# Cross-attention and FFN: scores and maxima as pairs of 64-row matmuls, operands in projection layout, softmax sums inverted by way of DMA

## The reference

```python
q, k, v = layer_norm(x, g_norm) @ Wq, context @ Wk, context @ Wv      # 16 heads of 64
k, v = [null_k, k], [null_v, v]                                       # 1602 keys
attn = softmax(q @ k.T / 8)                                           # per head, 2048 x 1602
out = layer_norm((attn @ v) @ Wout, g_out)
x = x + out
h = relu(s0 * [y, -y] @ W0) * 2; h = relu(s1 * h @ W1) * 2; h = s2 * h @ W2     # y = layernorm(x)
x = x + h
```

## Time and profile before

| | us |
|---|---|
| runs | 1573.2, 1545.63, 1547.75 (median 1547.75) |
| profiled execution | 1543.19, of it span 1541.2 |
| head, up to the first scores | 128.5 |
| pair 0 / pairs 1 to 6 / pair 7 | 150.1 / 883.1 (147.2 each) / 133.5 |
| tail | 246.0 |
| busy: PE, DVE, POOL, ACT | 1478.7, 1030.3, 779.2, 707.2 |

### The profile page before, as it was taken

The page is one execution under the profiler, slowest core; times in us unless marked ns, Lnnn a source line. Parts: engine busy times, 40 slices in busy tenths (PEclk is TensorE's granted clock), DMA queues, the critical chain, the costliest instruction groups (busy, mean ns, idle before and its releaser), DMA issues.

```text
span 1541.2 us, 20363 instructions
## 1 busy us (share of the span) xinstructions
PE 1478.7 (96%) x6068; PEld 735.0 (48%) x6068; DVE 1030.3 (67%) x1288; ACT 707.2 (46%) x1169; POOL 779.2 (51%) x657
## 2 busy tenths in 40 slices
PE   5888999999999999999999999999999998999998
PEld 3334444444444434444444444444443443878777
DVE  7785677577757866776687578757876838544542
ACT  3324544644464446445544554465445535232242
POOL 3004667566757655666567566656675645101100
PEclk9998999999999999999999999999999999999999
DMA  5222200120020002000200120012002302101000
GB/s 162 76 76 78 57 8 8 34 59 8 11 59 31 8 16 79 8 8 21 72 8 14 25 64 7 15 34 58 8 8 87 123 0 69 55 14 54 14 14 14
DMA packets 46947, 60.23 MB, mean 39 GB/s; under 512 B 4721, under 2 KB 32308, under 8 KB 46836
## 3 DMA queue, kind: packets, MB, share of 16 engines
q1 hardware_dynamic: 46836, 58.92, 12.9%
HBM read 26.27 MB, written 17.30 MB: 28 GB/s over the span
## 4 chain that ended last, share of the span: by engine, by line
PE 89%; DVE 5%; issue 2%; ACT 2%; POOL 1%; DMA 0%; DVEq 0%; SPq 0%; ACTq 0%; POOLq 0%
PE ps_o L1247 26%; PE ps_s L1269 17%; PE ps_s L1270 12%; PE ps_side L1331 10%; PE ps_side L1184 9%; PE ps_side L1172 3%; PE ps_s L1292 3%; PE ps_side L1206 2%; PE ps_side L1162 1%; PE ps_side L1163 1%; DVE mxh L926 1%; PE ps_o L1146 1%; PE ps_side L1193 1%; PE ps_o L1148 1%; DVE khl L915 1%
## 5 line engine op out<-in xcount | busy, mean ns | idle before, releaser
L423 POOL TENSOR_TENSOR acc<-acc,prob 128x512 f32<-128x512 f32 x522 | 670.4, 1302 | 307.5 <-ACT prob L778 300.5
L778 ACT ACTIVATE prob<-ps_s,keybias 128x512 f32<-128x512 f32 x832 | 526.4, 683 | 526.0 <-PE ps_s L1270 482.2
L926 DVE TENSOR_REDUCE mxh<-ps_side 128x2 f32<-128x804 f32 x512 | 485.6, 991 | 122.0 <-PE ps_side L1184 119.2
L1247 PE MATMUL ps_o<-prob,vp 128*64 128x512 f32 x1664 | 448.3, 616 | 0.0
L1269 PE MATMUL ps_s<-qdup,khl 128*128 128x512 f32 x832 | 373.4, 449 | 7.5 <-issue 5.4
L1269 PEld LDWEIGHTS ps_s<-qdup,khl 128*128 128x128 f32 x832 | 156.0, 188 | 364.4 <-issue 261.5
L1270 PE MATMUL ps_s<-qrest,krest 128*128 128x512 f32 x832 | 329.3, 396 | 0.0
L423 DVE TENSOR_TENSOR acc<-acc,prob 128x512 f32<-128x512 f32 x182 | 166.9, 919 | 58.5 <-ACT prob L778 48.5
L1184 PE MATMUL ps_side<-khl,qdup 64*128 64x402 f32 x1024 | 170.5, 401 | 11.5 <-DVE mxh L926 4.3
L1270 PEld LDWEIGHTS ps_s<-qrest,krest 128*128 128x128 f32 x832 | 157.2, 189 | 18.8
L1247 PEld LDWEIGHTS ps_o<-prob,vp 128*64 128x64 f32 x1664 | 84.9, 135 | 140.8 <-issue 81.1
(11 more groups left out here) (130 smaller groups left out, 1041.7 us busy)
## 6 DMA issues: line engine op xcount, KB each, us to landing
qdup<-qdup SPq DMA_DIRECT2D x64, 128.0 KB, 2.3
o_scratch<-onorm SPq DMA_DIRECT2D x32, 256.0 KB, 2.1
otb<-o_scratch SPq DMA_DIRECT2D x4, 2048.0 KB, 7.8
v_scratch<-vsb SPq DMA_DIRECT2D x13, 512.0 KB, 3.2
krest<-khl SPq DMA_DIRECT2D x16, 416.0 KB, 5.1
vp<-v_scratch SPq DMA_DIRECT2D x8, 832.0 KB, 7.4
xs<-in_x SPq DMA_DIRECT2D x4, 512.0 KB, 6.6
xres<-in_x SPq DMA_DIRECT2D x1, 2048.0 KB, 11.1
```

Of the source, the lines that this page charges most:

```text
L423: eng.tensor_tensor(a, so_far, prob[g][s % RING][:, :], ALU.add).then_inc(sum_done[g], 1)
L778: act.activation(prob[g][s % RING][:, :], ps_s[g][:, :], ACT.Exp, bias=keybias[:, kt:kt + 1], scale=SCALE).then_inc(p_made[g], 1)
L926: dve.reduce_max(mxh[:, qt % QH, :, quarter], ps_side[slot][:, :, 0:MXW], AX.X).then_inc(side_free[slot], 1)
L1247: last = pe.matmul(ps_o[qb % 2][hi_rows(g), :], vp[u][:, kt, hi_rows(g)], prob[g][s % RING][:, :], start=(kt == 0), stop=(kt == KT - 1))
```

## The change

**Operands.** `qdup`, `qrest`, `khl`, `krest` become `qh`, `ql`, `kh`, `kl`: 128 partitions as the projection leaves them, head 0 on rows 0-63, head 1 on rows 64-127. One instruction rounds both heads and one makes both rests; the DMAs that copied halves are gone. The subtraction of the maximum becomes a product of `one_sel` and `shift`.

**Scores.** A step's scores are now four pairs of 64-row matmuls (rounded by rounded, rest of k, rest of q, maximum), each pair one head on each half of the rows, into one of two PSUM tiles of two banks. ACT makes both heads' `prob` in one instruction on 128x1024, in a ring of eight.

**Order.** A **cycle** is two steps: maxima ("pre"), scores of step 2c, values of step 2c-2, maxima ("mid", in 12 of the 26 cycles), scores of step 2c+1, maxima ("post"), one spare job, values of step 2c-1. The maxima of query blocks 1 to 3 are now made in the pair that uses them, those of block 0 and six of block 1 in the pair before: the head holds 22 of the 64, pair 7 holds 42 where it had none.

**PSUM.** The maxima have one tile, `ps_x`; K, Q, MX and L jobs use the bank of `ps_o` that collects no values at the time.

**Sums.** POOL adds nine `prob` tiles a block on 128x1024, DVE tiles 4, 5 and 6 in two additions; POOL adds DVE's part. The sums go to DRAM, come back as 128x8, are inverted, go out and come back spread over the rows; ACT copies the values out of PSUM.

```diff
-            plan[c + 1].append(("Q", c))
-            plan[4 + c if c else 0].append(("K", c))
...
+K_AT, Q_AT, MX_AT, L_AT, C_AT = (3, 5, 6, 8), (11, 12, 16, 19), (23, 4, 10, 17), (9, 15, 22, 2), (18, 19)
+SPLIT_WQ_AT = 6
+SA_THREE = {2, 3, 5, 6, 8, 9, 11, 12, 15, 16, 19, 22}
+RECIP_AT, NORM_AT = (11, 17, 24, 4), (13, 19, 0, 6)
+HEAD_SA = 6
...
+    stream = [(0, qb, j) for qb in range(1, QB) for j in range(16)][HEAD_SA:]
+    if not last:
+        stream += [(1, 0, j) for j in range(16)] + [(1, 1, j) for j in range(HEAD_SA)]
...
+        for where in ("pre", "mid", "post") if c in SA_THREE else ("pre", "post"):
...
+D_TILES = (4, 5, 6)
...
-        ps_side = [psum(f"ps_side{r}", [P, 2, 512]) for r in range(2)]
+        ps_x = psum("ps_x", [P, 2, 512])
...
-                        pe.matmul(ps_s[g][:, :], khl[u][g][:, ks], qdup[u][g][:, qs], start=True, stop=False)
-                        pe.matmul(ps_s[g][:, :], krest[u][g][:, ks], qrest[u][g][:, qs], start=False,
-                                  stop=True).then_inc(s_made[g], 1)
...
+                for left, right, cols in ((kh[u], qh[u], ks), (kl[u], qh[u], ks), (kh[u], ql[u], ks), (one_sel, shift[u], slice(0, P))):
+                    for g in range(2):
+                        last = pe.matmul(ps_s[s % S_BUFS][:, g, :], left[rows(g), cols], right[rows(g), qs],
+                                         start=(left is kh[u] and right is qh[u]), stop=(left is one_sel))
...
+            def maxima(j, job, pair):
+
+                dn, qb, i = job
+                n, _, u = pair if pair is not None and dn == 0 else after(pair)
+                qt, quarter = i // 4, i % 4
+                at = x_count(j, pair)
+                if pair is not None or at > 0:
+                    pe.wait_ge(x_free, at)
...
+                dve.wait_ge(x_made, at + 1)
+                dve.reduce_max(mxh[:, :, qt, quarter], ps_x[:, :, 0:MXW], AX.X).then_inc(x_free, 1)
...
+                dve.tensor_tensor(acc_d[:, :, :], prob[slot(u, s)][:, :, :], prob[slot(u, s + 1)][:, :, :],
+                                  ALU.add).then_inc(sums_d, 1)
...
+                        if c == (KT * qb + D_TILES[1]) // 2 + 1:
+                            add_first(n, u, qb, first)
+                        if c == (KT * qb + D_TILES[2]) // 2 + 1:
+                            add_second(n, u, qb)
...
+    for j in range(16):
+        order += [("SA", 0, j), next(values)]
+        if j in (5, 11):
+            order += queries(2 if j == 5 else 3)
+    for j in range(HEAD_SA):
+        order += [("SA", 1, j), next(values)]
+        if j == 0:
+            order += [("MX", 0)]
+    order += [job for job in values]
```

More of the change, by code:

```diff
@@ new lines, in plan_pair @@
+def plan_pair(first, last):
+    plan = [{"pre": [], "mid": [], "post": [], "F": [], "L": []} for _ in range(CYCLES)]
+    stream = [(0, qb, j) for qb in range(1, QB) for j in range(16)][HEAD_SA:]
+    if not last:
+        stream += [(1, 0, j) for j in range(16)] + [(1, 1, j) for j in range(HEAD_SA)]
+    x = 0
+    for c in range(CYCLES):
+        for where in ("pre", "mid", "post") if c in SA_THREE else ("pre", "post"):
+            if x < len(stream):
+                plan[c][where].append((x, stream[x]))
+                x += 1
+    y = 0
+    for c in range(CYCLES):
+        jobs = []
+        if not last:
+            jobs += [("K", 1, i) for i in range(4) if K_AT[i] == c] + [("Q", 1, i) for i in range(4) if Q_AT[i] == c]
+        for qb in range(QB):
+            if MX_AT[qb] == c and not (last and qb == 0):
+                jobs.append(("MX", 1 if qb == 0 else 0, qb))
+        for job in jobs:
+            plan[c]["F"].append((y, job))
+            y += 1
+        if last and c in C_AT:
+            plan[c]["F"].append((x, ("C", 0, C_AT.index(c))))
+            x += 1
+        for qb in range(QB):
+            if L_AT[qb] == c and not (first and qb == QB - 1):
+                plan[c]["L"].append((y, ("L", -1 if qb == QB - 1 else 0, qb)))
+                y += 1
+    return plan, x, y
@@ L107, in plan_head @@
     order += queries(0) + queries(1)
[L108 to L122, removed]
+    for j in range(16):
[7 more added lines that the diff above has]
+    order += [job for job in values]
+    out, x, y = [], 0, 0
     for job in order:
@@ L125, in plan_head, with spare_bank, y_before, freed_by @@
             out.append((None, job))
-        else:
[L127 to L154, removed]
+        elif job[0] == "SA":
+            out.append((x, job))
+            x += 1
+        else:
+            out.append((y, job))
+            y += 1
+    return out, x, y
+HEAD, HEAD_X, HEAD_Y = plan_head()
+def spare_bank(c):
+    ended = sum(c > (KT * (qb + 1) - 1) // 2 + 1 for qb in range(QB - 1))
+    if c == 0:
+        return 0, -1
+    return 1 - ended % 2, ended
+def y_before(plan, step):
+    c = step // 2 + 1
+    jobs = [job for i in range(c) for job in plan[i]["F"] + plan[i]["L"]] + (plan[c]["F"] if step % 2 else [])
+    return sum(job[0] != "C" for _, job in jobs)
+D_TILES = (4, 5, 6)
+def freed_by(s):
+    qb, kt = s // KT, s % KT
+    if kt in D_TILES:
+        return "D", SUMS_D * qb + (1 if kt < 6 else 2)
+    return "P", SUMS_P * qb + {0: 1, 1: 1, 2: 2, 3: 3, 7: 4, 8: 5, 9: 7, 10: 8, 11: 9, 12: 10}[kt]
 def plan_chain():
@@ new lines, in spare, with sums @@
+                    n = 0 if pair is None else pair[0] + dn
+                    pe.wait_ge(mx_made, blocks(n, qb) + 1)
+                    pe.transpose(ps[0:8, 0:P], mx[:, qb % 2, :], ident[:, :]).then_inc(y_job_made, 1)
+                else:
+                    _, dn, qb = job
+                    sums(ps, pair[0] + dn, qb)
+            def sums(ps, n, qb):
+                pe.wait_ge(sums_p, 1 + SUMS_P * (blocks(n, qb) + 1))
+                for g in range(2):
+                    last = pe.matmul(ps[rows(g), :], ones[:, :], acc[qb % 2][:, g, :], start=True, stop=True)
+                last.then_inc(y_job_made, 1)
```

948 lines of the change are left out of this document (511 added, 437 removed).

## The result

| | before | after |
|---|---|---|
| median of the runs, us | 1553.5 | 1602.8 (1601.9 to 1603.3) |
| profiled execution, of it span | 1543.2, 1541.2 | 1603.1, 1601.2 |
| mean granted clock of TensorE | 0.993 | 0.975 |

A forecast was written before the change was run, and what follows sets the result against it. The prediction took TensorE, busy 96% of the span, as the bound. Middle pairs +36.0, pair 0 +13.7, pair 7 +16.8, head -25.1 and tail +3 made +44.4 on 1543.2, written as 1588 us, range 1505 to 1640 (its own case 1562 to 1612).

The forecast's parts named there:

- Scores, maxima, mode changes: Middle pair on TensorE: scores unchanged at 0.235 us a pair, maxima -5.8 us, K, Q and MX jobs +2.5.
- Rivals B: Score matmuls on TensorE: pairs cost 0.213 us, -5.4 us a pair, giving 1547 us; chance 0.08.
- C: Score matmuls on TensorE: weight loads show, 0.10 us each, +167 us, giving 1755 us; chance 0.04.
- E: 64-row matmul pairs on TensorE: the two halves run one after the other; given no chance.
- One tile: Maxima in a single PSUM tile: TensorE waits 0.40 us behind mid, 0.14 behind post; +6.2 us a middle pair.
- DVE's additions: VectorE's additions delay reductions, mainly in cycle 11, partly locked by POOL: +5.0 us a middle pair, bounds 1 and 13.
- Pair's start: First steps of a middle pair: waits for projections and their splits vanish, -1.9 us.
- Pair 0: First pair: +8, less 3.0 us for weights, plus 8.8 waiting for the last value projection's copy, store and load: +13.7.
- Pair 7: Last pair: 42 new maxima 8.0 us, one-tile waits 4.6, additions 3.0, MX and output jobs 1.2: +16.8.
- Head: Before pair 0: 42 fewer maxima, -38.4 us; the 22 left at 1.52 each, +13.3; together -25.1.
- Tail: After the last pair: POOL's last block of sums ends later, less the inversion's former cost: +3 us.
- Rival A: VectorE's reductions never late: one-tile and addition terms vanish, -85 us, giving 1503 us; chance 0.16 in full, 0.19 by half.

The follow-up runs named there:

- e1: Changed kernel with VectorE's additions taken away, POOL adding all 12 tiles of a block: 1538.3 us, 0.988 of the kernel before.
- e3: e1 with maxima reductions reading only 201 of the 402 columns of each head: 1481.8 us, 0.951 of the kernel before.
- e2: Changed kernel with maxima reductions reading only 201 of the 402 columns of each head: 1541.3 us, 0.991 of the kernel before.
- e9: e1 with last-pair conversions of w0 and w2 in cycles 16 and 17, POOL's second roots behind its last addition, w1 after y: 1531.7 us.
- e7: e1 with last-pair conversions of w0 and w2 in cycle 20 and the last four y tiles of block 0 made by POOL: 1537.8 us.
- e5: Changed kernel with VectorE's second addition one cycle later in each pair's second and fourth block: 1552.3 us, 0.997 of the kernel before.

## Why the prediction was right, and where it was short

The side was right (slower by 2.6% forecast, 3.3% measured), and 1602.8 lies in the likeliest case's own range, 1562 to 1612. The side rests on VectorE's additions: e1, without them, is at 0.988 of the time before. The profiled executions differ by 60.0 us for 44.4. The middle pairs miss by 16, pair 7 by 6.4 and the tail by 2.3; the head (-6.0) and pair 0 (-3.0) miss the other way, and that these took 9 us back is luck. By its steps:

*Scores, maxima, mode changes.* Pairs of scores start 0.232 apart (0.235 taken), an SA job ahead of scores adds 0.18 (0.29 to the next start in e3, but the first score pair then takes 0.23 for 0.34; 0.19 taken). Rivals B, C and E fall. Without additions a middle pair is 146.9 (e1), 0.3 under before; the forecast without its additions is 1.0 over. These terms are right to 1.3 us a pair. The sentence of the Trainium skill in "TensorE: Matmul & The Clock Gate", Part 3, by which a load overlaps running matmuls only where its row group differs, is not borne out: the next pair's loads start with the running pair, into the same rows, and the pairs stay 0.232 apart. The same section also lets a load go ahead when it targets the background weight buffer, which the forecast did not weigh; the trace does not contradict that.

```profile
97.38 0.40 PE L1381 MATMUL ps_s<-qh,kh 64*128 64x512 f32 x2
97.38 0.19 PEld L1381 LDWEIGHTS ps_s<-qh,kl 64*128 64x128 f32 x2
97.61 0.40 PE L1381 MATMUL ps_s<-qh,kl 64*128 64x512 f32 x2
```

*One tile.* +6.2 a pair forecast, 6.6 measured by e3 against e1. Right, place by place: 0.40 and 0.14 forecast, 0.41 and 0.16 measured.

*DVE's additions* is the step that was short: +5.0 forecast, 8.9 measured by e1. The place was right (cycle 11), and the wait there near it, 3.26 us of idle TensorE for +3.4. Missing was the stretch at 1.2 GHz that comes with such a wait: in pair 3 TensorE came back at 0.50 for 3.35 us and had 0.86 over the next 8, and in most pairs the clock fell again behind cycle 24's wait. Cycle 11's excess of 5.1 is about 3 of waiting and 2 of clock. Over six pairs these 3.9 us are 23, more than the miss of 16 there. The traces part the wait from the clock, since the clock does not fall each time. In e2 TensorE idles 2.84 us in cycle 11 of pair 2 and of pair 3 alike; these are the two cycles:

```profile
455.53:466.41 10.88, 8.04 (x39) 4.18 (x38) 6.71 (x6) 2.83 (x3) 9.40 (x5) 0.84 0.01 2
605.07:614.42 9.35, 6.51 (x39) 3.34 (x37) 6.58 (x6) 2.83 (x3) 7.95 (x4) 1.00 0.01 2
```

With the clock at full the cycle is 2.9 us over e3's 6.42, the wait alone; with the fall it is 1.5 us longer. It fell in three of the six middle pairs, which have that wait alike, and the clock stays at full in the middle pairs of e1, where no wait is over 1.3 us. What decides between the two outcomes at one length of wait is open. The lock itself, which the Trainium skill states in "SBUF — State Buffer", "Who interferes with whom", the runs confirm: 1.23 alone, 3.26 behind a whole POOL instruction, up to 2.2 behind half a one.

*Pair's start.* Right: cycles 0 and 1 of e1 last 4.81, as others of their kind do.

*Pair 0*: +10.7 for +13.7, of two errors that partly cancel. The additions cost 8.4 (e1) for 5.0. The rest is +2.3 for +8.7: the wait for `vp` is there, but 3.5 us and not 8.8. It was issued at 100.29 and landed by 104.7, 4.4 us, where I took the median of 7.4, and the copy ahead of its store began 0.9 us before the first scores. The pair also begins at full clock (1.00 from 97.38 to 104.70), where the kernel before has 0.50 for its first 8.5 us; the forecast had it at half again.

```profile
100.29 0.35 SPq L528 DMA_DIRECT2D vp<-v_scratch  x1
...
104.71 0.67 PE L1381 MATMUL ps_s<-qh,kh 64*128 64x512 f32 x2 [3.52 <-DMA vp<-v_scratch]
```

*Pair 7*: +23.2 for +16.8. Its cycle 11 lasts 15.8: the conversions of w0 and w2 stand behind the locked addition, ahead of a reduction. I had left them out; before, that pair had no maxima to be late. e9 prices them at 5.8. The additions cost 7.5 there (e1) for 3.0, and the rest, maxima and their waits, 9.9 for 13.8, which hid part of both.

```profile
1253.72 3.19 DVE L1031 TENSOR_TENSOR acc_d<-acc_d,prob 128x1024 f32<-128x1024 f32 x1
...
1256.83 2.28 DVE L1130 TENSOR_TENSOR w<-k0raw 128x2048 fp32r<-128x2048 uint8 x1
...
1259.03 3.36 DVE L1131 TENSOR_SCALAR w<-k2raw 128x2048 fp32r<-128x2048 uint8 x1
...
1263.41 0.70 PE L1267 MATMUL ps_x<-kh,qh 64*128 64x402 f32 x2 [8.61 <-DVE mxh L995]
```

*Head*: -31.1 for -25.1. The 22 maxima go at 1.54 each as forecast, but begin at 39.8 and not at 47.3; the earlier start I left out. *Tail*: +5.3 for +3. TensorE waits 8.4 us for the four locked y tiles, but POOL's last addition ends with them, and e7 shows that the tail waits for that too; no run parts the two.

*Rival A* (no reduction late) is not what happens, yet e3 shows what it was worth: with both terms gone the time is 1482. Its gain of 85 us would have been 121; 26 of the difference are the additions, and 9 the short reductions, which quicken the head too.

## What to carry to other kernels

An engine that works half the time can still be the one that sets the pace: look at what stands ahead of each instruction that the bottleneck waits for, and count not its own length but that of the longest instruction it can be locked behind. Cut such work or give it away (64 us here), or spread it so that no two long pieces stand ahead of one hand-over (50 us); then put work of one kind on TensorE side by side, in that order, since the new order gained 63 us without the late additions and 25 with them. When a wait appears or goes, count the clock with it.

## What the runs showed of the hardware that was not expected

- A VectorE instruction with one SBUF input is held up by POOL too, and by whole instructions whatever its own size: four of 256 elements, 1.38 us alone, took 9.88 beside four POOL additions of 2.45. The section of the Trainium skill named above ("Who interferes with whom") has it that `tensor_scalar` can enter a two-port mode of VectorE and then takes the same lock. The conversion of w2, a `tensor_scalar` too, agrees: 2048 elements in 1.21 us in e5, where an addition takes 1.22 for 1024, and 3.36 in after. Of the y tiles no row tells the mode. The forecast applied the rule to the additions alone. Reductions that read PSUM were not: 995 ns in after, 997 in e1 with POOL busy 955 us for 817.
- After 3.3 us in which it was idle, TensorE did the next 3.35 us of work at a granted clock of 0.50. With the same idle time of 2.84 us in cycle 11 of e2, the clock fell in some pairs and stayed at full in others (0.84 and 1.00 over the cycle), a difference of 1.5 us.
- Changing between kinds of matmuls costs more than the one slow start: S V S V against S S V V was 0.36 us in a cycle of 4.64, and the values' own spacing is part of it (0.47 and 0.52 us for the first and last pair of a group, 0.42 between).
